# Head attention with its split tokens turned by DMA transposes from the third job on

## The reference, cut to what matters

```
def _L0_attn_a_ref(x):                    # x: layer norm of the input, B=2, S=2048, D=256
    qkv = x.reshape(B, S, 16, 16).transpose(0, 2, 1, 3)
    q = k = v = qkv                       # no projections: the tokens are query, key and value
    w = einsum('bhqd,bhkd->bhqk', q, k) / sqrt(16)
    w = softmax(where(causal, w, min), axis=-1)
    return einsum('bhqk,bhkd->bhqd', w, v).transpose(0, 2, 1, 3).reshape(B, S, D)

x = x + _L0_attn_a_ref(_layernorm(x))     # this stage
x = x + _L0_ffn_ref(_layernorm(x), ...)   # top 2 of 8 experts
x = x + _L0_attn_b_ref(_layernorm(x), ...)
x = x + _L0_ffn_ref(_layernorm(x), ...)
```

## Time and profile before

| | |
|---|---|
| median of 3 runs | 1648.09 us (1646.58 to 1648.27) |
| the profiled execution, its own time | 1646.33 us |
| its span in the profile | 1644.6 us |
| head attention within it | 0 to 523 us |
| busy: PE, ACT, DVE, POOL | 1589.9, 985.9, 1079.5, 360.7 us |
| mean granted TensorE clock | 0.999 of 2.4 GHz |

### The profile page before, as it was taken

How to read it: one execution, slowest core, us unless ns; L and a number is a source line. 1 busy time by engine, 2 the same in 40 slices (tenths; PEclk the granted TensorE clock), 3 DMA queues, 4 the chain that set the end, 5 groups by cost and what they waited for, 6 DMA issues and landing times.

```text
span 1644.6 us, 30645 instructions
## 1 busy us (share of the span) xinstructions
PE 1589.9 (97%) x11755; PEld 869.9 (53%) x11755; DVE 1079.5 (66%) x2159; ACT 985.9 (60%) x1260; POOL 360.7 (22%) x466
## 2 busy tenths in 40 slices
PE   6999999999999999999999999999999899999998
PEld 2222222222222666666675666666666566666666
DVE  7533454454343975786656689868899897577554
ACT  6999999999988433443336545555445443353322
POOL 2012122122022000011105345544444400011000
PEclk9999999999999999999999999999999999999999
DMA  4013234000040003011110001000001201411100
GB/s 140 17 36 107 79 117 166 23 15 16 21 123 1 14 14 116 14 20 21 20 20 14 1 2 20 17 17 1 1 1 40 78 14 28 128 27 33 33 14 27
DMA packets 96559, 65.52 MB, mean 40 GB/s; under 512 B 55887, under 2 KB 91294, under 8 KB 96414
## 3 DMA queue, kind: packets, MB, share of 16 engines
q1 hardware_dynamic: 96414, 63.55, 14.1%
HBM read 38.88 MB, written 4.19 MB: 26 GB/s over the span
## 4 chain that ended last, share of the span: by engine, by line
PE 63%; ACT 16%; issue 11%; DVE 8%; POOL 1%; DMA 0%; ACTq 0%; DVEq 0%; POOLq 0%
ACT a_probs L782 15%; PE f_ypsum L1047 7%; PE f_ypsum L1049 7%; PE f_ypsum L1048 7%; PE f_h L1047 7%; PE f_h L1049 7%; PE f_h L1048 7%; PE a_out L539 4%; PE d_outs L1047 3%; PE d_outs L1049 2%; PE d_outs L1048 2%; PE a_scores L916 2%; DVE d_dist L2070 2%; PE d_banks L1047 2%; PE d_banks L1049 2%
## 5 line engine op out<-in xcount | busy, mean ns | idle before, releaser
L782 ACT ACTIVATE a_probs<-a_scores 128x1024 f32<-128x1024 f32 x544 | 500.2, 1207 | 10.4 <-PE a_scores L916 10.4
L1410 ACT ACTIVATE f_gelu<-f_h,f_bcol,s_more 128x512 f32<-128x512 f32 x256 | 198.9, 777 | 406.4 <-PE f_h L1049 391.7
L539 PE MATMUL a_out<-a_probs,a_values 128*32 128x512 f32 (+3 forms) x2560 | 294.9, 542 | 6.6 <-ACT a_probs L782 5.5
L1465 DVE TENSOR_SCALAR f_hh<-f_gelu,f_gates_scaled 128x512 f16<-128x512 f32 x256 | 136.5, 533 | 183.0 <-ACT f_gelu L1410 182.3
L1923 ACT ACTIVATE d_score<-d_dist,d_nksq,s_more 128x512 f32<-128x512 f32 x128 | 104.1, 813 | 194.8 <-DVE d_dist L2070 193.0
L1047 PE MATMUL f_ypsum<-f_w,f_hh 128*128 128x256 f16 x768 | 209.3, 273 | 0.0
L1048 PE MATMUL f_ypsum<-f_w,f_hh 128*128 128x256 f16 x768 | 209.3, 273 | 0.0
L1049 PE MATMUL f_ypsum<-f_w,f_hl 128*128 128x256 f16 x768 | 209.3, 273 | 0.0
L1467 DVE SCALAR_TENSOR_TENSOR f_hl<-f_gelu,f_gates_scaled,f_hh 128x512 f16<-128x512 f32 x256 | 193.3, 755 | 9.1
L916 PE MATMUL a_scores<-a_moving,a_fixed 64*128 64x512 f16 (+3 forms) x1280 | 184.6, 354 | 10.2 <-ACT a_probs L782 3.7
L796 POOL TENSOR_SCALAR_AFFINE_SELECT a_probs<-a_probs 128x256 f32<-128x256 f32 (+1 forms) x224 | 98.0, 452 | 423.9 <-ACT a_probs L782 421.5
(11 more groups left out here) (258 smaller groups left out, 2700.5 us busy)
## 6 DMA issues: line engine op xcount, KB each, us to landing
f_raw<-in_L_ffn_W SPq DMA_DIRECT2D x16, 1024.0 KB, 7.9
f_raw<-in_L_ffn_W SPq DMA_DIRECT2D x24, 512.0 KB, 7.3
a_fixed<-a_moving SPq DMA_DIRECT2D x60, 96.0 KB, 2.3
x<-in_L_attn_a_x SPq DMA_DIRECT2D x7, 512.0 KB, 6.1
out<-x SPq DMA_DIRECT2D x7, 512.0 KB, 3.1
f_raw<-in_L_ffn_W SPq DMA_DIRECT2D x12, 256.0 KB, 3.5
a_fixed<-a_moving SPq DMA_DIRECT2D x60, 32.0 KB, 2.0
f_early_raw<-in_L_ffn_W SPq DMA_DIRECT2D x4, 256.0 KB, 3.7
```

What stands on the lines that cost most here:

```text
L539: mm = pe.matmul(spare[32 * j:32 * j + 32, i % 2, skip:skip + w], values[:, G % 2, kt + tile, j, :], probs[:, u % UR, j % 2, col:col + w], ...
L782: act.activation(probs[:, u % UR], scores[:, 2 * (u % SR):2 * (u % SR) + 2, :], ACT.Exp, scale=HD ** -0.5)\
L1410: act.activation(gel[:, n % HR, :], hps[:, n % 2, :], ACT.Gelu, bias=mix.bcol[:, q, FT * e + j:FT * e + j + 1], scale=pr.scales.hidden)\
L1465: dve.tensor_scalar(hh[:, n % HR, :], gel[:, n % HR, :], gate, None, ALU.mult).then_inc(s_hh, 1)
```

## The change

From job 2 on, PE turns nothing and DVE places nothing. SP issues one DMA transpose of the eight blocks of `split_m`, straight into `moving`, waits for it, and issues the four DMAs of `copy_fixed` as before. The new semaphore `s_turned` takes the place of `s_emov` (for SP and for PE's first step of an output) and of `s_tmov` (for DVE's `halves`). The operands have a new layout: [partition, tile of 128 tokens, pair of heads, 128] instead of [partition, pair of heads, 2048 tokens], so that the eight blocks follow each other; PE now reads 512 columns of `moving` as four runs of 128, and the four DMAs move one run of 2 KB in each partition instead of two of 1 KB. Jobs 0 and 1 go the old way into the new layout. The tables of turns are gone. SP's queue gets 30 transposes.

```diff
-        moving, fixed = ([first, sb(f"a_{n}1", [P, GH // 2, S], F16)] ...
+        moving, fixed = ([first, sb(f"a_{n}1", [P, TILES, GH // 2, P], F16)] ...
-        TURN_AT = {15: (0, (0, 1)), 16: (0, (2, 3)), 17: (1, (0,)), 18: (1, (1,)), ...
-        FIRST_TURN_AT = {11: (3, (0, 1)), 12: (3, (2, 3)), 19: (4, (0,)), ...
+        def turned(engine, job):
+
+            if job < BY_ENGINES:
+                engine.wait_ge(s_emov, job + 1)
+            else:
+                engine.wait_ge(s_turned, 16 * (job - BY_ENGINES + 1))
+        def tiles_of(operand, job):
+
+            G, cc = outputs[job]
+            return operand[G % 2][:, TPC * cc:TPC * (cc + 1)]
...
             def copy_fixed(job):
-                sp.wait_ge(s_emov, job + 1)
+                turned(sp, job)
...
-                        sp.dma_start(fixed[G % 2][a:a + rows, :, cut], moving[G % 2][b:b + rows, :, cut]).then_inc(s_efix[job % 2], 16)
+                        sp.dma_start(tiles_of(fixed, job)[a:a + rows], tiles_of(moving, job)[b:b + rows]).then_inc(s_efix[job % 2], 16)
+            def turn(job):
+                sp.wait_ge(s_lo, job + 1)
+                sp.dma_start(tiles_of(moving, job).rearrange("p t r n -> p (t r) n"),
+                             split_m[:, job % 2].rearrange("p t h i j e -> p (t h i j e)"), transpose=True).then_inc(s_turned, 16)
             load_batch(pr, sp, 0)
+            turn(BY_ENGINES)
             copy_fixed(BY_ENGINES)
             load_batch(pr, sp, 1)
...
             for job in range(BY_ENGINES + 1, CHUNKS * NG):
+                turn(job)
                 copy_fixed(job)
...
             def halves(job):
                 if job >= 2:
-                    dve.wait_ge(s_tmov, job - 1)
+                    turned(dve, job - 2)
...
             copy_out(0)
-            place(2)
             statistics(2)
...
                 if kt == 0 and kind in ("full", "first"):
-                    pe.wait_ge(s_emov, job + 1)
+                    turned(pe, job)
...
-                                mm = pe.matmul(scores[...], fixed[G % 2][head, a, k0:k0 + P],
-                                               moving[G % 2][head, a, q0:q0 + w], start=True, stop=True)
+                                mm = pe.matmul(scores[...], fixed[G % 2][head, kt + tile, a, :],
+                                               moving[G % 2][head, q0:q0 + w // P, a, :], start=True, stop=True)
...
-                if n == 5:
-                    turn(2)
...
-                if n in FIRST_TURN_AT:
-                    turn(*FIRST_TURN_AT[n])
...
-                if GS <= n < GS * (NG - 1) and n % GS in TURN_AT:
-                    job, tiles = TURN_AT[n % GS]
-                    turn(CHUNKS * (n // GS + 1) + job, tiles)
```

More of the change, by code:

```diff
@@ L443, in head_attention @@
         weights.place_scratch(ctx)
-        moving, fixed = ([first, sb(f"a_{n}1", [P, GH // 2, S], F16)] for n, first in (("moving", moving), ("fixed", fixed)))
+        moving, fixed = ([first, sb(f"a_{n}1", [P, TILES, GH // 2, P], F16)] for n, first in (("moving", moving), ("fixed", fixed)))
         split_f = sb("a_split_f", [P, 2, TPC, GH, 4, HD], F16)
@@ L458, in head_attention @@
         routing = Routing(pr, 0, spare[:, 1, :])
[L459 removed]
+        (s_ones, s_xn, s_hi, s_lo, s_hi_f, s_lo_f, s_tmov, s_emov, s_tfix, s_pfix, s_scores, s_exp, s_mask, s_pv, s_ocopy,
          s_oturn, s_rden, s_onorm, s_added) = pr.sems(
[L461 removed]
+            "a", "ones", "xn", "hi", "lo", "hi_f", "lo_f", "tmov", "emov", "tfix", "pfix", "scores", "exp", "mask", "pv",
             "ocopy", "oturn", "rden", "onorm", "added")
+        s_turned, = pr.sems("a", "turned")
         outputs = [(0, 0), (1, 0)] + [(G, c) for G in range(NG) for c in range(CHUNKS) if (G, c) not in ((0, 0), (1, 0))]
@@ L494, in head_attention @@
         LAG = 2
[L496 to L513, removed]
         BY_ENGINES = 2
@@ L616, in place @@
             def place(job):
-                G, cc = outputs[job]
-                cut = slice(cc * CHUNK, (cc + 1) * CHUNK)
                 dve.wait_ge(s_tmov, job + 1)
-                dve.tensor_copy(moving[G % 2][:, :, cut], as_pairs(turned(job))).then_inc(s_emov, 1)
+                dve.tensor_copy(tiles_of(moving, job).rearrange("p t r n -> p r t n"), as_pairs(spare[:, job, :])).then_inc(s_emov, 1)
             def place_fixed():
                 dve.wait_ge(s_tfix, 2)
-                dve.tensor_copy(fixed[1][:, :, 0:CHUNK], as_pairs(fixed_turned[1])).then_inc(s_pfix1, 1)
+                dve.tensor_copy(tiles_of(fixed, 1).rearrange("p t r n -> p r t n"), as_pairs(fixed_turned[1])).then_inc(s_pfix, 1)
             def copy_out(i):
@@ L709, in _ @@
                     scales.scan(dve, SCAN_AT[i], mix)
[L710 to L714, removed]
                 if i == GATHER_AT:
@@ L851, in last_group, with turn @@
                     reads[0].append((mix.s_b2w, 1))
[L853 to L862, removed]
+            def turn(job):
+                reads[job].append((s_emov, job + 1))
+                pe.wait_ge(s_lo, job + 1)
+                for t in range(TPC):
                     for r in range(GH // 2):
[L864 to L867, removed]
+                        mm = pe.transpose(spare[:, job, :].bitcast(F16)[:, (r * TPC + t) * P:(r * TPC + t + 1) * P],
+                                          split_m[:, job, t, 2 * r:2 * r + 2].rearrange("p a i j e -> p (a i j e)"), pr.ident16[:])
+                mm.then_inc(s_tmov, 1)
             def turn_fixed(job):
@@ L2140, in hybrid_block @@
                 mix.parts = [early[:, i] for i in range(mix.EARLY)]
-                moving, fixed = (pr.sb(layer)(f"a_{n}0", [P, 2, S], F16) for n in ("moving", "fixed"))
+                moving, fixed = (pr.sb(layer)(f"a_{n}0", [P, TILES, 2, P], F16) for n in ("moving", "fixed"))
                 from_heads = head_attention(pr, block, inputs, cols, w, mix, moving, fixed)
```

19 lines of the change are left out of this document (5 added, 14 removed).

## The result

| | before | after |
|---|---|---|
| median of 12 runs each | 1648.24 us (1646.51 to 1651.73) | 1652.57 us (1648.53 to 1655.41) |
| profiled execution, its span | 1646.33, 1644.6 us | 1653.25, 1651.6 us |

The ratio of the runs is 1.0026, 95% interval 1.0019 to 1.0034: the change costs 4.3 us. 1651.2 had been forecast, from 1646.8 to 1655.0.

A forecast was written before the change was run, and what follows sets the result against it. ACT's exponentials, 0.904 us each, were taken to bound the stage. Late operands 5.2, plus clock 0.8, less 2.9 from removed turns, gave +3.1 us: 1651.2 us against the median of 1648.09, range 1646.8 to 1655.0.

The forecast's parts named there:

- job 2 late: At job 2: the eight-block transpose takes 4.0 us, so the operand is ready 2.5 us late (0.9 to 3.3).
- at output 3, job 2 and clock included: From output 3 on: everything 5.2 us later, job 2's 2.5 included, plus 0.8 us for PE's slow clock.
- gain in the middle: Exponentials of G = 1 to 6: without PE's turns, bumps in their starts go, winning 2.9 us (2.4 to 3.8).
- G = 7: Late in the kernel: no term of its own; the rest from 523 us on was said only to shift.
- The floor of 0.904 us: ACT's exponentials: starts 0.904 us apart were taken as the pace, 491.8 us for 544, untouchable by changes on PE and DVE.
- Rival 4: Bumps in the exponentials' starts aren't the turns' and stay, leaving only the loss: +6 us, 1654; chance 0.05.
- The 0.5 for the gather: Router's gather on DVE: its second half no longer waits for turns and follows the first at once, winning 0.5 us.
- Job 3: At job 3: SP last, transpose issued at 38.4 behind the loads, landing at 43.3; 5.2 us later, job 2 included.
- Clock: PE's clock falls after idling at the waits for jobs 2 and 3: 0.8 us over both, 0 to 1.4.
- The layout costs nothing: PE reading four runs of 128 instead of 512: no cost, covered by 0.28 us a step.
- Later operands in time: Jobs after 3: DVE splits each tens of us ahead of first use, so their operands are not late.
- Longer exponentials would mean a disturbance: ACT: longer exponentials named as a sign of being wrong, meaning that DMA writes disturb ACT.

The follow-up runs named there:

- e1: Changed kernel, but job 2 turned by PE and placed by DVE as before, DMA transposes from job 3 on: 1649.69 us, ratio 1.0011 to the kernel before.
- e2: Changed kernel, but jobs 2 and 3 turned by PE as before, the other 28 by DMA: 1648.01 us, ratio 1.0005 to the kernel before.
- e10: Changed kernel without any edit, profiled a second time: one run, 1651.01 us.
- e8: Kernel before without any edit, profiled a second time: one run, 1648.04 us.
- e7: Kernel before with products three steps behind the scores instead of two (LAG = 3): 1649.82 us, ratio 1.0006 to the kernel before.
- e9: Kernel before with each turn of jobs 8 to 31 done twice by PE: 1651.56 us, ratio 1.0021 to the kernel before.
- e3: Changed kernel with 13 more unused PE matmuls ahead of each wait for job 2's and job 3's operands: 1653.27 us, ratio 1.0034 to the kernel before.
- e4: Changed kernel with job 3's transpose and copies ahead of the bulk loads in SP's queue: 1651.75 us, ratio 1.0022 to the kernel before.
- e12: Kernel before with one edit in G = 7, DVE's copy_out ahead of the two tokens' norms: 1643.76 us, ratio 0.9977 to the kernel before.

## Why the prediction was right, point by point

The time lay in the range, and the sign was right for the reason given: the first two operands come late, and e1 and e2, which turn them by PE again, take the loss away. That the size came out so near is in part luck, since errors in both directions stand against each other. The second pair of profiles is e10 against e8.

| step | forecast | first pair | second pair |
|---|---|---|---|
| job 2 late | +2.5 us | +1.86 | +1.92 |
| at output 3, job 2 and clock included | +6.0 | +4.64 | +4.62 |
| gain in the middle | -2.9 | -0.58 | -0.03 (0.58 less 0.56 of slow clock) |
| G = 7 | 0 | +1.2 | 0.0 |
| sum | +3.1 | +5.26 | +4.57 |

The medians of the whole lie 4.3 apart.

- **The floor of 0.904 us** is the step that failed. Starts were taken for the pace, and 0.0127 us a unit over 68 units, 0.86 a group, was read as bumps of the turns. Rival 4 (the bumps aren't the turns') had been given 0.05, and that is what happened: e2 and e7 show the pace unmoved, and e9 that turns cost only beyond the cushion. In the middle 0.58 us was won instead of 2.9. The 0.5 for the gather was mis-sized too; DVE's order alone gave under 0.1.
- **Job 2** was mis-sized: 4.0 us taken, 3.17 measured. The reason was the guess that the issue doubles with the blocks; it grew from 1.19 to 1.31 us.
- **Job 3**: "SP last, issued directly behind the last load" did not hold in the changed kernel (38.81 against 37.65), but it held in e3, at full clock. The backlog was real, 0.9 us by e4. With 43.3 forecast for the operand and 42.75 measured, this step was right in size by luck, from two errors: a later split than thought (38.79 against 37.5) and a shorter landing (3.94 us against 4.9).
- **Clock**: +0.8 forecast, 1.8 at job 2. It could not simply be added to the rest: e3 took it away and output 3 came 0.07 us sooner, since the transpose, issued 1.5 us sooner, landed no sooner behind the loads. e10 shows the same without e3's extra matmuls (issued 0.4 sooner, landed 0.2 later). How much of e3's 5.4 us was backlog and how much the instruction packet is open.
- **The layout costs nothing**: right for the pace, which is 0.9167 in every profile with it but e3's. For the first jobs no run tests it alone.
- **Later operands in time**: right; ACT has no gap from 43.23 to 468.48 (in e10 it has one, at 45.79, behind the slow clock).
- **Longer exponentials would mean a disturbance**: wrong as a sign. They grew by 77 ns, and the pace stayed: scores that came further ahead of ACT.
- **G = 7** was called a mere shift. There PE idles 2.8 us in both kernels, and how long the clock stays down behind it varies: about 3.4 us before (479.8 to 483.2), about 7 after (482 to 489). From the start of the row of 15 exponentials to that of the row of 29 it took 32.96 and 32.93 us in the two profiles before, 34.16 and 32.91 in those after, so the 1.2 us come in some executions only.

What stays open: why job 2's slow clock comes more often with DMA turns, and how much of the 4.3 us of the medians it is. The two pairs of profiles end the stage 5.26 and 4.57 us apart, their whole times lie 6.9 and 3.0 apart, the medians 4.3, and the runs of one kernel spread over 5.2 to 6.9 us, several times a slow stretch of 1.7.

## What to carry to other kernels

Before calling late starts a loss, compare ends over a long row: if the time from end to end is that of a row without a gap, the engine lost nothing, however its starts lie. Here a transfer that replaced work of PE was free where its operand was needed tens of microseconds later, and made it late by 1.9 us and more where it was needed at once, so leave the first jobs with the engines. And look for the one long idle time of PE before trimming its many short instructions: moving one copy on DVE gave 4 us (e12), taking 28 jobs' turns from PE 0.6 (e2).

## What the runs showed of the hardware

- In a timeline an engine's starts and ends can run at different paces: exponentials of 128x1024 from PSUM started 0.904 us apart for 26 in a row and ended 0.9167 apart over 464.
- A DMA transpose of eight 128x128 blocks in f16 issued in 1.24 to 1.36 us when undisturbed, one of four in 1.19, and landed after 3.0 to 3.2 us against 2.4 (the slowest of the 30 took 7.9). By the Trainium skill one 128x128 block in bf16 takes 1309 ns (VectorE: DVE Perf Modes, "The three transpose paths"). Eight f16 blocks in one instruction took 3.1 us in the median, so the time is not 1309 ns for each.
- PE idled 3.65 us up to 26.51, and its clock stood at 0.50 (1.2 GHz) from 24.8 to 31.6 us, though PE was busy 5.09 of these 6.80 us. Sixteen products took 1.87 us in it (28.59 in the chain), against 1.07 for sixteen in e3, where the clock stayed up.
- The same program had its clock down at other places from execution to execution: 24.8 to 31.6 us in one profile of the changed kernel, 26.7 to 30.1 and 43.8 to 47.2 in the other.
